# A fused macaron block in fp32 on one core: new work orders at the start, in the middle and at the end, a first column taken from PSUM, epsilon on GpSimd, a shorter Newton iteration

## The reference

```
def ffn(x):
    prev = x shifted by one token, 0 for the first token of a row
    xr, xk = mu_r*x + (1-mu_r)*prev, mu_k*x + (1-mu_k)*prev
    return sigmoid(xr @ W_r.T) * (relu(xk @ W_k.T)**2 @ W_v.T)
def attn(x):                     # 16 heads of 16, no mask, no softmax
    q, k = relu(x @ Wq.T)/4, relu(x @ Wk.T)/4;  v = x @ Wv.T;  u = silu(x @ Wu.T)
    out = q @ (k.T @ v)          # one 16x16 matrix per head and sequence
    out = out / max(rms(out over the head), 1e-12) * u
    return out @ Wo.T
x = x + 0.5*ffn(layernorm(x));  x = x + attn(layernorm(x));  x = x + 0.5*ffn(layernorm(x))
```

## Time and profile before

| | |
|---|---|
| median of three runs | 350.19 us (348.17 to 351.12) |
| the profiled execution | 346.65 us, of which the span from the first to the last instruction is 344.9 us |
| TensorE busy | 322.9 us, 94% of the span |
| VectorE, ScalarE, GpSimd busy | 261.8, 212.1 and 141.7 us |
| HBM read and written | 6.29 and 4.19 MB |

### The profile page before, as it was taken

One profiled execution on the slowest core, in us unless ns is written; L12 is line 12 of the kernel. 1 busy time (PEld: TensorE's weight loads), 2 busy tenths in 40 slices (PEclk: granted clock), 3 DMA queues, 4 the chain that ended last, 5 costly groups with the idle time before them and its releaser, 6 DMA issues.

```text
span 344.9 us, 5499 instructions
## 1 busy us (share of the span) xinstructions
PE 322.9 (94%) x1906; PEld 285.2 (83%) x1906; DVE 261.8 (76%) x676; ACT 212.1 (62%) x390; POOL 141.7 (41%) x148
## 2 busy tenths in 40 slices
PE   6879979999999999999999967999999999999886
PEld 6678868889888888899888956879898999889765
DVE  4969894885848758888584799267899999994563
ACT  3896656828659268284173065068685959667871
POOL 3486914616237144172144123012281817373541
PEclk9999999999999999999999999999999999999999
DMA  7940000000000000000000000000010101011103
GB/s 240 352 141 0 3 0 0 3 1 2 0 0 2 1 2 1 0 2 0 2 0 0 3 0 0 3 0 2 1 61 2 61 2 63 2 61 61 43 20 122
DMA packets 11034, 10.83 MB, mean 31 GB/s; under 512 B 768, under 2 KB 11008, under 8 KB 11008
## 3 DMA queue, kind: packets, MB, share of 16 engines
q1 hardware_dynamic: 10176, 9.96, 8.9%
q10 hardware_dynamic: 832, 0.53, 0.5%
HBM read 6.29 MB, written 4.19 MB: 30 GB/s over the span
## 4 chain that ended last, share of the span: by engine, by line
PE 75%; DVE 9%; ACT 9%; issue 4%; POOL 2%; DVEq 0%; ACTq 0%; POOLq 0%
PE psX L1053 8%; PE psK L1002 8%; PE psK L891 5%; PE psRV L891 5%; PE psRV L962 5%; PE psRV L893 5%; PE psRV L892 5%; PE psK L892 5%; PE psK L893 5%; PE psX L891 4%; PE psX L892 4%; PE psX L893 4%; PE psA L910 2%; PE psRV L1071 2%; ACT mix L413 2%
## 5 line engine op out<-in xcount | busy, mean ns | idle before, releaser
L658 DVE SCALAR_TENSOR_TENSOR mix<-psA,mu,mix 128x512 f32<-128x512 f32 x64 | 43.7, 745 | 11.8 <-ACT mix L413 11.4
L300 POOL TENSOR_TENSOR mix_k_lo<-mix,mix_k_hi 128x512 fp32r<-128x512 f32 x32 | 40.6, 1290 | 23.2 <-ACT mix_k_hi L422 23.2
L413 ACT ACTIVATE mix<-psA,one_mu 128x511 f32<-128x511 f32 x64 | 39.4, 698 | 0.8 <-PE psA L910 0.8
L891 PE MATMUL psRV<-ffn_hi,mix_r_hi 128*128 128x256 f32 x128 | 36.5, 285 | 0.0
L893 PE MATMUL psRV<-ffn_hi,mix_r_lo 128*128 128x256 f32 x128 | 35.8, 279 | 0.0
L892 PE MATMUL psRV<-ffn_lo,mix_r_hi 128*128 128x256 f32 x128 | 35.7, 279 | 0.0
L400 ACT ACTIVATE xn<-xs,shiftA,rstdA 128x256 f32<-128x256 f32 x62 | 32.7, 593 | 3.7 <-POOL shiftA L287 3.7
L285 POOL TENSOR_TENSOR rstdA<-var_epsA,minus_half 128x4 f32<-128x4 f32 x16 | 16.6, 1035 | 38.2 <-DVE neg_meanA L618 19.4
L1053 PE MATMUL psX<-wo,g_t 128*128 128x256 f32 x128 | 29.1, 381 | 2.9 <-ACT g_t L487 2.9
L217 POOL TENSOR_TENSOR gout<-gout,head_rn 128x512 f32<-128x512 f32 x8 | 12.5, 1566 | 46.5 <-DVE head_rn L758 46.5
L291 POOL TENSOR_TENSOR rstdB<-var_epsB,minus_half 128x4 f32<-128x4 f32 x8 | 8.1, 1009 | 56.6 <-DVE clampB L634 56.6
(11 more groups left out here) (130 smaller groups left out, 889.4 us busy)
## 6 DMA issues: line engine op xcount, KB each, us to landing
xs<-x_dram SPq DMA_DIRECT2D x7, 512.0 KB, 8.6
out_dram<-xs SPq DMA_DIRECT2D x7, 512.0 KB, 2.9
xs<-x_dram SPq DMA_DIRECT2D x4, 128.0 KB, 3.3
out_dram<-xs SPq DMA_DIRECT2D x4, 128.0 KB, 1.7
silu_u<-w_ffn_k_dram ACTq DMA_DIRECT2D x1, 256.0 KB, 3.1
silu_u<-w_ffn_r_dram ACTq DMA_DIRECT2D x1, 256.0 KB, 5.1
ffn_v_plain<-w_ffn_v_dram SPq DMA_DIRECT2D x1, 256.0 KB, 5.8
silu_u<-w_k_dram SPq DMA_DIRECT2D x1, 256.0 KB, 6.0
```

The source lines that it names most:

```text
L300: nc.gpsimd.tensor_tensor(mix_k_lo[:, h, :], mix[:, 0, h, :], mix_k_hi[:, h, :].bitcast(F32), ALU.subtract).then_inc(s_lo_k, 1)
L413: nc.scalar.activation(mix[:, rk, h, 1:BLOCK], psA[:, h, 0:BLOCK - 1], ACT.Copy, scale=one_mu[:, rk, h:h + 1]).then_inc(s_prev, 1)
L658: nc.vector.scalar_tensor_tensor(out=m, in0=psA[:, h, :], scalar=mu[:, rk, h:h + 1], in1=m, op0=ALU.mult, op1=ALU.add).then_inc(s_mix, 1)
L891: nc.tensor.matmul(dst, a_hi, b_hi, start=start, stop=False)
```

## The change

- **End.** In the stream of TensorE, iterations 13 and 14 put `transpose_a(n + 1)` ahead of `ffn_k(n)`; in iteration 12 `project_out(7)` goes behind `ffn_v2(12)`. ScalarE and VectorE follow: `previous(n + 1)` comes first in iterations 13 and 14, `add_attention(7)` and `stats_a(15)` move into iteration 13, and two of the four tiles of pass 15 are normalized on VectorE (`normalize_rest`).
- **Iteration without FFN.** `gram(6)` moves behind `transpose_a(8)` and `transpose_b(7)`, which change places; `attend(3)` moves ahead of `project_out(2)`. On VectorE `head_norms(2)` and `x2_low(7)` go ahead of `keep_g(6)` and `stats_a(9)`, and `gate_heads(3)` ahead of `add_attention(2)`.
- **kv.** `kv(0)` writes a half of `psA` and `kv(1)` a half of `psRV`, so that `ffn_k` doesn't wait for `mask_kv`.
- **Start.** Tiles 2 and 3 of block 0 are loaded by ScalarE's queue, the weights of k and r by SP's. In pass 0 both k mixes come first; the low parts of k and of the activation are made by VectorE, those of the k weights and of r by GpSimd. The column means of the attention weights (`weight_means`) move behind `ffn_k(0)`, with 20 idle transposes in place of 10. ScalarE runs `activate_k(0)` ahead of `normalize(1)`, and `normalize(3)` only behind the last `sigmoid_u` of iteration 1.
- **Everywhere.** `halo` holds (1-mu) times the last token, made by VectorE from PSUM (`next_column`) in place of the copy; ScalarE copies it to column 0. Epsilon is added by GpSimd, which makes the shift in two instructions; `stats_a(n)` waits for all of `scales_a(n - 1)`. The Newton part has 9 instructions in place of 12.

```diff
@@ SP and ScalarE queues
-            for t in range(TILES):
+            for t in (0, 1):
                 sp.dma_start(tile_row(xs, 0, t), x[t * P:(t + 1) * P, :]).then_inc(s_x0[t], 16)
+            sp.dma_start(raw_ffn[:, 0, :, :], weight_rows("ffn_k")).then_inc(s_w_in["ffn_k"], 16)
             load_x(1)
+            sp.dma_start(raw_ffn[:, 1, :, :], weight_rows("ffn_r")).then_inc(s_w_in["ffn_r"], 16)
...
+            for t in (2, 3):
+                act.dma_start(tile_row(xs, 0, t), x[t * P:(t + 1) * P, :]).then_inc(s_x0[t], 16)
@@ GpSimd, scales_a
-                pool.wait_ge(s_mvA, 2 * (n + 1))
+                pool.wait_ge(s_aggA, 4 * (n + 1))
+                nc.gpsimd.tensor_scalar(var_epsA[:], meanvarA[:, :, 1], 1.0, LN_EPS, ALU.mult, ALU.add
+                                        ).then_inc(s_mvA, 1)
...
+                nc.gpsimd.tensor_tensor(mean_rstdA[:], meanvarA[:, :, 0], rstdA[:], ALU.mult).then_inc(s_lnA, 1)
+                pool.wait_ge(s_lnA, 3 * n + 2)
+                nc.gpsimd.tensor_scalar(shiftA[:], mean_rstdA[:], -1.0, 0.0, ALU.mult, ALU.add).then_inc(s_lnA, 1)
@@ GpSimd, start
             scales_a(0)
+            pool.wait_ge(s_ffn_hi, 1)
+            nc.gpsimd.tensor_tensor(ffn_lo[:, 0, :, :], ...)
             scales_a(1)
-            k_low(0)
-            weights_low((0, 1))
-            act_low(0)
+            (r low parts of pass 0)
+            act_squares(0)
+            scales_a(2)
+            weights_low((0,))
             k_low(1)
-            scales_a(2)
-            weights_low((2,))
+            weights_low((1, 2))
@@ ScalarE
+            def first_column(n):
+                stage, b = FFN[n]
+                act.wait_ge(s_halo, n + 1)
+                nc.scalar.activation(mix[:, :, :, 0], halo[:, 0 if b % BB == 0 else stage, :, :],
+                                     ACT.Copy).then_inc(s_prev, 1)
...
             mix_high(0, 1)
+            activate_k(0)
             normalize(1)
             ffn_weight_high(2)
             att_weight_high(0)
-            att_weight_high(1)
-            activate_k(0)
             previous(1)
             sigmoid_r(0, 0)
             sigmoid_r(0, 1)
+            att_weight_high(1)
...
+            for n in range(13, LAST):
+                previous(n + 1)
+                activate_k2(n)
+                sigmoid_r(n, 0)
+                sigmoid_r(n, 1)
+                mix_high(n + 1, 0)
+                mix_high(n + 1, 1)
                 if n + 2 <= LAST:
-                    normalize(n + 2)
+                    normalize(n + 2, tiles=(0, 1))
@@ VectorE
+            def next_column(n):
+                nc.vector.tensor_tensor(halo[:, FFN[n][0], :, :], one_mu[:],
+                                        psA[:, :, BLOCK - 1].unsqueeze(1).to_broadcast([P, 2, HALVES]),
+                                        ALU.mult).then_inc(s_halo, 1)
...
             add_attention(1)
+            gate_heads(2)
+            head_norms(2)
+            x2_low(7)
             keep_g(6)
             stats_a(9)
-            gate_heads(2)
-            head_norms(2)
-            x2_low(7)
-            first_column(8)
             mix_current(8)
             projections(7, 8)
+            gate_heads(3)
             add_attention(2)
@@ TensorE
-            keep_clock_up(10)
+            keep_clock_up(20)
+            pe.wait_ge(s_ffn_lo[0], 1)
+            ffn_k(0)
             weight_means(0)
-            pe.wait_ge(s_ffn_lo, 1)
-            ffn_k(0)
             weight_means(1)
...
-            gram(6)
             attend(2, [(s_gu, 4)])
             q_of(6, [(s_x2, 4)])
+            transpose_a(8, [(s_gu, 6)])
             transpose_b(7)
-            transpose_a(8, [(s_gu, 6)])
+            gram(6)
             pe.wait_ge(s_gacc, 7)
             k_and_u(7)
             transpose_g(2, [(s_silu, 30)])
+            attend(3, [(s_halo, 10)])
             project_out(2)
             gram(7)
-            attend(3, [(s_halo, 10)])
             q_of(7, [(s_x2, 6)])
-            kv(1)
+            kv(1, [(s_gated, 16)])
...
+            for n in range(13, LAST):
+                transpose_a(n + 1)
+                ffn_k(n, [(s_relu, 2 * n)])
+                ffn_r(n)
+                ffn_v2(n)
```

More of the change, by code:

```diff
@@ L135, in macaron @@
         s_tA = sem("s_tA")
-        s_col0 = sem("s_col0")
         s_prev = sem("s_prev")
@@ L463, in sigmoid_u @@
                         act.wait_ge(s_att_lo, 3)
-                        act.wait_ge(s_ffn_lo, 3)
+                        for done in s_ffn_lo:
+                            act.wait_ge(done, 1)
                 nc.scalar.activation(tile_row(silu_u, a, t), (psX, psK)[t // 2][:, t % 2, D:2 * D], ACT.Sigmoid,
@@ L491, in _ @@
             ffn_weight_high(0)
+            normalize(0, tiles=(0, 1))
             ffn_weight_high(1)
-            normalize(0, tiles=(0, 1))
-            previous(0)
-            mix_high(0, 0)
+            first_column(0)
+            act.wait_ge(s_one_mu, 1)
+            for h in range(HALVES):
+                previous_part(0, 0, h)
+            for h in range(HALVES):
+                mix_high(0, 0, (h,))
+                previous_part(0, 1, h)
             mix_high(0, 1)
+            activate_k(0)
             normalize(1)
@@ L560, in _ @@
             normalize(9)
-            for n in range(8, 16):
+            for n in range(8, 13):
                 j = n - 5
@@ L656, in mix_current @@
                     for rk in range(2):
-                        m = mix[:, rk, h, :]
-                        nc.vector.scalar_tensor_tensor(out=m, in0=psA[:, h, :], scalar=mu[:, rk, h:h + 1], in1=m,
-                                                       op0=ALU.mult, op1=ALU.add).then_inc(s_mix, 1)
+                        mix_one(n, rk, h)
                 if HALVES - 1 in halves:
-                    nc.vector.tensor_copy(halo[:, stage, :], psA[:, :, BLOCK - 1]).then_inc(s_halo, 1)
+                    next_column(n)
@@ L850, in _ @@
             add_attention(1)
-            keep_g(6)
-            stats_a(9)
             gate_heads(2)
@@ L856, in _ @@
             x2_low(7)
-            first_column(8)
+            keep_g(6)
+            stats_a(9)
             mix_current(8)
             projections(7, 8)
+            gate_heads(3)
             add_attention(2)
@@ L870, in _ @@
                     gate_ffn(n - 1, 1)
-                if j < NB:
-                    head_norms(j)
-                if 8 < n and n + 2 <= LAST:
+                head_norms(j)
+                if n > 8:
                     stats_a(n + 2)
-                first_column(n + 1)
                 mix_current(n + 1, (0,))
@@ L1004, in gram, with kv @@
                 last.then_inc(s_gt, 1)
-            def kv(batch):
+            def kv(batch, free):
+                for s, v in free:
+                    pe.wait_ge(s, v)
                 pe.wait_ge(s_gacc, BB * (batch + 1))
@@ L1106, in _ @@
                 q_of(i - 1, [(s_silu, 4 * (i - 1) + 2)])
-            kv(0)
-            ffn_k(5, [(s_gacc, 4), (s_kvbd, 1)])
-            transpose_a(6)
+            kv(0, [(s_halo, 7)])
+            ffn_k(5, [(s_gacc, 4)])
+            transpose_a(6, [(s_kvbd, 1)])
             transpose_b(4)
```

234 lines of the change are left out of this document (123 added, 111 removed).

## The result

The changed kernel takes 338.06 us (median of 4, 337.72 to 338.20); the kernel before, measured beside it, 349.18 us (347.79 to 351.12). The ratio is 0.968 [0.962, 0.973]: faster by 11.1 us. Its profiled execution took 338.2 us with a span of 336.5, against 346.65 and 344.9 before: 8.4 us. The forecast was 340.2 us (336.5 to 345.5).

The account below looks back on a forecast made before the run. TensorE bounds the kernel, its idle time nearly all in three short stretches. Gains of 3.8 + 3.9 + 0.7 + 1.6 = 10.0 us off the median give 340.2 us (336.5 to 345.5).

Parts of the forecast that it names:

- end: Last iterations: earlier transposes and `ffn_v2(12)` cover TensorE's marked waits; 3.8 us gained, from 2.5 to 4.5.
- iteration without FFN with kv(1): Middle: reordered work fills TensorE's waits and `kv(1)` no longer holds `ffn_k(8)`; 3.9 us gained, from 2.2 to 5.
- kv(0): At `ffn_k(5)`, which no longer waits for the mask: 0.7 us gained, from 0.5 to 0.8.
- start: `gram(0)` starts at 46.2 to 46.4 us instead of 47.95: 1.6 us gained, from -0.5 to 3.
- The 0.7 us that the prediction took off at the end: New TensorE wait at `transpose_a(15)` for `xn`, since ScalarE needs about 10.7 us and TensorE wants it after 10.
- rival (b): Waits in the middle and at the start move rather than go: 5.4 us gained, 344.8 us; chance 0.2.
- (a): The forecast itself holds: whole kernel at 338 to 343 us; chance 0.62.
- The step on the longer chain: GpSimd's added small instructions lengthen the chain from statistics to `xn` by about 0.3 us, mattering at `normalize(8)`.
- Rival (c): GpSimd's new small instructions take as long as the power, `xn` comes 2 us later: 345 us; chance 0.07.
- Rival (e): Slower: TensorE waits at `ffn_k(0)` or `transpose_a(15)` until its clock falls to 1.2 GHz; 368 us at 28 us; chance 0.03.
- the Newton part: Three instructions fewer per block, 6 us of VectorE in all, counting only in the iteration without FFN.
- The rule of the Trainium skill: VectorE instructions with two SBUF inputs contend with GpSimd's SBUF reads; three holds would take the start's gain to nothing.

Follow-up runs that it names:

- run 3: The changed kernel with the old order of the end (iterations 12 to 15) back on all engines: 341.99 us.
- run 1: The changed kernel with ScalarE normalizing all four tiles of pass i + 2 behind the last `sigmoid_u` in iterations 2 to 5: 335.94 us.
- run 2: The changed kernel with epsilon and the negated mean made by VectorE again, GpSimd keeping the power and one product: 336.75 us.
- run 4: The changed kernel with the old order of the iteration without FFN on TensorE and VectorE, Newton part still short: 340.97 us.
- run 5: The kernel before with 24 idle transposes ahead of `k_and_u(7)` and 14 ahead of `project_out(2)`, filling its two long middle waits: 348.85 us.
- run 9: The changed kernel with `normalize(3)` back between the sigmoids of iteration 1, two tiles ahead of the last `sigmoid_u`: 342.04 us.
- Run 8: The changed kernel with three more instructions in the Newton part, 12 instead of 9, their results unread: 338.20 us.
- Run 7: The changed kernel with `stats_a(9)` ahead of `keep_g(6)` on VectorE, and only the third tile of `k_and_u(7)` waiting for `keep_g(6)`: 336.22 us.
- run 10: The changed kernel with VectorE's `r_low(2)` moved behind the last `silu` of iteration 1: 336.09 us.

## Why the prediction was right, and where not

**The result and its reason were right.** The change works on the three short stretches where TensorE waited. Term by term, predicted and read from the two profiled executions: end 3.8 and 3.9, iteration without FFN with kv(1) 3.9 and 3.9, kv(0) 0.7 and 0.8, start 1.6 and 1.7. Undoing the end alone (run 3) costs 3.9 us. The 0.7 us that the prediction took off at the end (10.7 less 10 us; its text says 0.6) were 0.35. So rival (b), that the waits move rather than go, is refuted for the end and the middle. What it named is there (three waits on VectorE and ScalarE), but they hold 2.3 us in place of 5.4. VectorE has 57.4 us of work from 230 to 302 us (58 predicted). `next_column` was never held (0.141 to 0.151 us in all 16); this group of the changed kernel has the copy's price, as the prediction took:

```profile
L686 DVE TENSOR_TENSOR halo<-one_mu,psA 128x4 f32<-128x4 f32 x16 | 2.4, 147 | 0.0
```

**That the number came so near is in part luck.** The profiled execution gained 8.4 us, 1.6 less than the sum of 10.0, while the 3.5 us between it and the median, carried over as a constant, had vanished. The two misses have opposite signs and leave 340.2 against 338.06, at the lower edge of the 338 to 343 us of (a).

**The step on the longer chain failed, by 1.9 us.** The sentences were that "the chain from statistics to `xn` grows by about 0.3 us" and "Where it matters is `normalize(8)`". The prices of the small instructions were right; the groups of GpSimd:

```profile
L299 POOL TENSOR_TENSOR rstdA<-var_epsA,minus_half 128x4 f32<-128x4 f32 x16 | 16.6, 1041 | 5.7 <-ACT xn L425 2.9 <-POOL var_epsA L293 2.8
...
L303 POOL TENSOR_SCALAR shiftA<-mean_rstdA 128x4 f32<-128x4 f32 x16 | 4.3, 266 | 1.4
...
L293 POOL TENSOR_SCALAR var_epsA<-meanvarA 128x4 f32<-128x4 f32 x16 | 3.7, 234 | 35.9 <-DVE meanvarA L665 35.0
```

Rival (c) is out: 0.23 and 0.27 us, not 1. What was missed is the queue. GpSimd is still busy with the low part of k when the statistics are ready, so VectorE's 0.33 us had run beside it and saved nothing when they went. All that GpSimd got lies on the path: 0.37 us from the start of epsilon to the start of the power, 0.35 from the product to the shift, and a shift of 0.51 us in this pass, 0.19 in most. That last one ends with VectorE's `r_low(4)`, which had begun before it:

```profile
87.52 1.28 DVE L701 TENSOR_TENSOR mix_r_lo<-mix,mix_r_hi 128x512 fp32r<-128x512 f32 x2
```

In the passes beside it the product or the shift is stretched in the same way (0.41, 0.51 and 0.75 us), while the shorter chain before was through with 0.20. And ScalarE's `normalize` stands ahead of the last `sigmoid_u` of every steady iteration, not only of pass 8. Runs 1 and 2 take the loss away from either end.

**The clock was misjudged; it hid 2.7 us of gain.** Rival (e) rested on "a wait of 2.93 us left the clock at its full level". That is true of the one execution that the profile shows, and it was taken for a property of the kernel. The gap between that execution and the median, 3.5 us, stood in the prediction as an unexplained constant. Runs 4, 5 and 9 show what it was: falls to 1.2 GHz behind waits, each 1.7 us, and by the mean clock two or three in most executions of the kernel before (0.985 of 349.4 us is 10.5 us at half speed, three falls). With the long waits shortened all four executions of the changed kernel stand at 1.000, and the constant is gone: 338.06 rather than 340.2.

**In the middle one item was costed wrongly inside a right sum.** VectorE was to be the bound behind `k_and_u(7)`, the Newton part among its work. Run 8 shows that Newton is worth nothing there, since VectorE stands ahead of `keep_g(6)` for 1.30 us. The prediction's own times have this gap (VectorE is through at 202.9, `gram(6)` at 203.9), but it was given no price. Run 7, which fills it and narrows TensorE's wait for `keep_g(6)`, gains 1.8 us.

**At the start the end point was right, the way there partly.** `gram(0)` came at 46.23 (46.2 to 46.4 predicted). With `normalize(3)` left early it comes at 48.27 (run 9): with the rest of the change in place this move is worth 2.0 us, and without it the new head and GpSimd's longer chain together stand 0.3 us behind the kernel before. `ffn_r`'s weights took 7.3 us to land, not 5.8, and ScalarE waited for them until 10.01 us (needed by 9.9). The wait of 1.3 us that was left to ScalarE (1.58 measured) was not ScalarE's alone: run 10 takes all of it away on VectorE.

The rule of the Trainium skill (SBUF, "Who interferes with whom") that was weighed for this place did show. VectorE's `r_low(1)`, two instructions with two SBUF inputs, took 3.46 us instead of about 1.3, beside two GpSimd instructions with two SBUF inputs:

```profile
29.79 3.46 DVE L701 TENSOR_TENSOR mix_r_lo<-mix,mix_r_hi 128x512 fp32r<-128x512 f32 x2
...
29.28 3.42 POOL L340 TENSOR_TENSOR att_lo<-silu_u,att_hi 128x512 fp32r<-128x512 f32 x2
```

In pass 0 `act_lo(0)` took 2.06 us instead of about 1.3, and `r_low(2)` 2.07 (run 10). The trace agrees with the rule in these three. Only the last, longer by 0.8 us, lies directly ahead of the last `silu` for which `gram(0)` waits, and the gain there was not eaten. For one SBUF input the prediction gave the rule without its exception, the 2-port perf modes: the epsilon addition, one SBUF input on VectorE, took 0.52 us in iteration 1 of the kernel before and 0.62 us in run 2, instead of 0.17. Whether these ran in such a mode no run here shows.

## What to carry to other kernels

An instruction moved to another engine is costed by that engine's queue and not only by its length. If the old engine did it beside the new engine's work, all of it is added, and the order of whoever consumes it has to be fitted again. If the profiled execution lies below the median, ask what it doesn't show. Read the mean granted clock of every execution before you subtract a gain from the median. Look for what is queued behind a wait (`stats_a(9)`) or ahead of a result for which the bound engine waits (`r_low(2)`): two such moves gave 3.8 of the last 6 us.
